# Graph attention layer on one core: the two column halves of an adjacency unit converted by one VectorE operation

## The reference

```python
xt = einsum('ni,hio->hno', x, W)                       # 8192 x 256 -> 4 heads x 64
src = einsum('hnf,hf->hn', xt, a[:, :64]);  dst = einsum('hnf,hf->hn', xt, a[:, 64:])
e = leaky_relu(src[:, :, None] + dst[:, None, :], 0.2)
attention = softmax(where(adj > 0, e, -inf), axis=2)
h_prime = einsum('hij,hjf->hif', attention, xt)
out = layernorm(x + h_prime.transpose(1, 0, 2).reshape(n, 256))
```

## Time and profile before

| | us |
|---|---|
| median of 3 runs | 2083.66 (2082.74 to 2085.49) |
| the profiled execution | 2083.11 |
| its span in the trace | 2081.3 |
| PE busy | 1982.0 (95%) |
| DVE busy | 1977.7 (95%) |
| ACT busy | 1955.4 (94%) |
| idle of ACT before signs (L539), total | 18.0 |
| idle of DVE before masks (L746), total | 41.1 |

### The profile page before, as it was taken

The page is one execution under the profiler, slowest core; times in us unless marked ns, Lnnn a source line. Parts: engine busy times, 40 slices in busy tenths (PEclk is TensorE's granted clock), DMA queues, the critical chain, the costliest instruction groups (busy, mean ns, idle before and its releaser), DMA issues.

```text
span 2081.3 us, 74808 instructions
## 1 busy us (share of the span) xinstructions
PE 1982.0 (95%) x33296; PEld 1949.5 (94%) x33296; DVE 1977.7 (95%) x2185; ACT 1955.4 (94%) x1983; POOL 142.1 (7%) x179
## 2 busy tenths in 40 slices
PE   7767999999999999999999999999999999999997
PEld 5567999999999999999999999999999999999997
DVE  3998999999999999999999999999999999999887
ACT  4477999999999999999999999999999999999995
POOL 0210000000020001000010000000010001001000
PEclk9889999999999999999999999999999999999998
DMA  8999999998988988989887979889988888834311
GB/s 295 331 369 380 293 279 264 264 249 236 253 239 248 271 246 232 254 236 285 237 257 227 282 234 254 240 244 274 252 238 245 266 256 230 229 89 125 88 49 42
DMA packets 289935, 498.59 MB, mean 240 GB/s; under 512 B 133008, under 2 KB 142224, under 8 KB 289616
## 3 DMA queue, kind: packets, MB, share of 16 engines
q1 hardware_dynamic: 285408, 477.96, 78.5%
q0 software_dynamic: 4080, 15.73, 2.3%
q10 hardware_dynamic: 128, 0.13, 0.0%
HBM read 438.83 MB, written 25.56 MB: 223 GB/s over the span
## 4 chain that ended last, share of the span: by engine, by line
ACT 48%; PE 35%; DVE 9%; issue 4%; DMA 3%; SPq 1%; POOL 0%; DVEq 0%; ACTq 0%; POOLq 0%
ACT big L539 46%; PE acc L1020 34%; DMA raw<-in_adj_dram 3%; DVE big L746 3%; DVE big L752 1%; DVE nat L660 1%; ACT big L581 1%; ACT big L587 1%; DVE nat L666 1%; DVE big L726 1%; PE acc L950 0%; DVE big L724 0%; DMA AT<-in_x_dram 0%; PE acc L960 0%; DVE AT L719 0%
## 5 line engine op out<-in xcount | busy, mean ns | idle before, releaser
L1020 PE MATMUL acc<-big 128*128 128x130 f16 x32768 | 1884.8, 220 | 45.0 <-DVE big L752 25.0
L1020 PEld LDWEIGHTS acc<-big 128*128 128x128 fp8e4 x32768 | 1871.3, 98 | 58.7 <-issue 57.1
L539 ACT ACTIVATE big<-big,d_all 128x1024 int8<-128x1024 f32 x1756 | 1848.7, 1152 | 18.0 <-PE acc L1020 17.9
L746 DVE SCALAR_TENSOR_TENSOR big<-big,AT 128x1024 uint32<-128x1024 uint32 x512 | 623.2, 1217 | 41.1 <-ACT big L539 38.9
L752 DVE SCALAR_TENSOR_TENSOR big<-AT,big 128x1024 uint32<-128x1024 uint32 x512 | 623.7, 1218 | 9.5 <-DVE big L746 0.5
L733 DVE TENSOR_SCALAR big<-big,d_all 128x1024 uint8<-128x1024 f32 x292 | 215.9, 746 | 0.0
L660 DVE TENSOR_SCALAR nat<-raw 128x2048 uint8<-128x2048 int32 x128 | 159.3, 1244 | 5.9 <-DMA raw<-in_adj_dram 5.6
L666 DVE TENSOR_SCALAR nat<-raw 128x2048 uint8<-128x2048 int32 x128 | 159.5, 1246 | 0.0
L483 POOL TENSOR_TENSOR wden<-big,ab 128x16 f32<-128x16 f32 x31 | 29.5, 950 | 886.2 <-DVE big L775 886.2
L673 DVE SCALAR_TENSOR_TENSOR nat<-nat 128x512 uint32<-128x512 uint32 x128 | 88.0, 688 | 0.0
L980 PE MATMUL acc<-big 128*128 128x256 f32 x256 | 62.1, 405 | 1.1 <-DVE AT L719 1.1
(11 more groups left out here) (64 smaller groups left out, 345.8 us busy)
## 6 DMA issues: line engine op xcount, KB each, us to landing
raw<-in_adj_dram SPq DMA_DIRECT2D x256, 1024.0 KB, 8.3
big<-v_parts SPq DMA_DIRECT2D x512, 260.0 KB, 6.6
v_parts<-big SPq DMA_DIRECT2D x16, 1040.0 KB, 7.1
big<-s_rows SPq DMA_DIRECT2D x32, 512.0 KB, 6.3
AT<-in_x_dram SPq DMA_DIRECT2D x16, 512.0 KB, 8.9
big<-in_x_dram POOLq DMA_DIRECT2D x8, 1024.0 KB, 11.2
out_dram<-big POOLq DMA_DIRECT2D x7, 1024.0 KB, 8.0
AT<-nat SPq DMA_TRANSPOSE x112, 8.7
```

The source lines that it names most:

```text
L539: return nc.scalar.activation(sgn[:, g % NB, :, b, :], sq[:, h % 2], ACT.Sign, bias=dflat[:, r:r + 1], scale=-1.0)
L746: nc.vector.scalar_tensor_tensor(out=word(sgn, g % NB), in0=word(sgn, g % NB), scalar=EDGE[g % 2], in1=edges(c, g), op0=ALU.bitwise_and, o ...
L1020: return nc.tensor.matmul(acc[:, k, o:o + 2 * VO], m[:, g % NB, t // 2, b, t % 2 * P:(t % 2 + 1) * P], Vr[:, v:v + 2 * VO], start=opens, s ...
```

## The change

From chunk 1 on (`all_columns`) one DVE operation with 4096 elements per partition converts both column halves of a unit, in step s = 4U+2. It writes 16 where an entry is above zero and 0 elsewhere, for both halves, into a new buffer `nat2` (in free words of `big`). Step 4U has no conversion any more. The merge stays in step 4U+3: it shifts the second half right by one bit (16 becomes 8) and ORs it into the first. The transposing DMA reads `nat2`. The waits on `raw` and on the earlier transpose, which `first_columns` had, now stand ahead of the one operation. The units of chunk 0 itself keep the two operations. The units for chunk 1, made during chunk 0, are converted in one operation at the place of the second one. New line numbers: mask 1 is L769, mask 2 L775, compares L756, the new conversion L685, the new merge L692, L775/L779/L805 are L798/L802/L828.

```diff
--- before.py
+++ after.py
@@ -83,6 +83,7 @@
         VR = 10240
         Vr = words(VR, 8320).bitcast(fp16)
         u = words(18560, 1040).rearrange("p (q v) -> p q v", v=VO)
+        nat2 = words(23696, 2048).bitcast(u8).rearrange("p (n v k) -> p n v k", n=2, v=2)
         y = [words(start, 2048).rearrange("p (t f) -> p t f", t=T) for start in (19600, 21648)]
 
 
@@ -189,14 +190,22 @@
         def edges(c, g):
             return AT[:, c % 2, g // 2]
 
-        def bits(c, n):
-            if c == 0:
-                return nat[:, n].rearrange("p (w z t) -> p z t w", z=2, t=2)
-            return nat[:, n].rearrange("p (z w t) -> p z t w", z=2, t=2)
+        def bits(n):
+            return nat[:, n].rearrange("p (w z t) -> p z t w", z=2, t=2)
 
         def columns(U, plane):
             k = U % 2 * 2
             return raw[:, k:k + 2, :, plane * CW:(plane + 1) * CW].rearrange("p z t w -> p z t w")
+
+        def bits_of_both(U):
+            return nat2[:, U % 2].rearrange("p v (z w t) -> p v z t w", z=2, t=2)
+
+        def columns_of_both(U):
+            k = U % 2 * 2
+            return raw[:, k:k + 2].rearrange("p z t (v w) -> p v z t w", v=2)
+
+        def joined(c, U):
+            return nat2[:, U % 2, 0] if c else nat[:, U % 2]
 
 
         def xt_of(n):
@@ -355,7 +364,7 @@
                 sp.wait_ge(merge_done, c * UN + U + 1)
                 sp.dma_start_transpose(AT[:, c % 2, U // 2, U % 2 * CW:(U % 2 + 1) * CW].bitcast(bf16)
                                        .rearrange("p (r i) -> p r i", i=P),
-                                       nat[:, U % 2].bitcast(bf16)).then_inc(turned[U % 2], 16)
+                                       joined(c, U).bitcast(bf16)).then_inc(turned[U % 2], 16)
 
             def load_x(g):
                 sp.dma_start(xg[g % NX], x_v[g]).then_inc(x_in[g % NX], 16)
@@ -648,30 +657,44 @@
 
 
 
-            def first_columns(c, U):
+            def raw_landed(c, U):
                 W = c * UN + U
                 dve.wait_ge(raw_in[U % 2 * 2], 16 * (W // 2) + 16)
                 dve.wait_ge(raw_in[U % 2 * 2 + 1], 16 * (W // 2) + 16)
+
+            def first_columns(U):
+                raw_landed(0, U)
+                if U > 1:
+                    dve.wait_ge(tp_done, U - 1)
+                dve.sem_inc(dve_passed, 1)
+                nc.vector.tensor_scalar(bits(U % 2), columns(U, 0), 0.0, BELOW[0], ALU.is_gt, ALU.add).then_inc(first_done, 1)
+
+            def last_columns(U):
+                if U:
+                    dve.wait_ge(merge_done, U)
+                nc.vector.tensor_scalar(bits(2), columns(U, 1), 0.0, BELOW[1], ALU.is_gt, ALU.add).then_inc(conv_done, 1)
+
+            def all_columns(c, U):
+                W = c * UN + U
+                raw_landed(c, U)
+                if W == UN:
+                    dve.wait_ge(*staged(NG - 1))
                 if W > UN + 1:
                     dve.wait_ge(turned[U % 2], 16 * ((W - UN) // 2))
-                elif W > 1:
-                    dve.wait_ge(tp_done, W - 1)
                 dve.sem_inc(dve_passed, 1)
-                nc.vector.tensor_scalar(bits(c, U % 2), columns(U, 0), 0.0, BELOW[0], ALU.is_gt, ALU.add).then_inc(first_done, 1)
-
-            def last_columns(c, U):
-                W = c * UN + U
-                if W:
-                    dve.wait_ge(merge_done, W)
-                nc.vector.tensor_scalar(bits(c, 2), columns(U, 1), 0.0, BELOW[1], ALU.is_gt, ALU.add).then_inc(conv_done, 1)
+                nc.vector.tensor_scalar(bits_of_both(U), columns_of_both(U), 0.0, 16.0, ALU.is_gt, ALU.mult).then_inc(conv_done, 1)
 
             def merge(c, U):
                 W = c * UN + U
-                dve.wait_ge(first_done, W + 1)
                 dve.wait_ge(conv_done, W + 1)
-                both = nat[:, U % 2].bitcast(u32)
-                nc.vector.scalar_tensor_tensor(out=both, in0=both, scalar=EDGE[0], in1=nat[:, 2].bitcast(u32),
-                                               op0=ALU.bitwise_and, op1=ALU.bitwise_or).then_inc(merge_done, 1)
+                both = joined(c, U).bitcast(u32)
+                if c:
+                    nc.vector.scalar_tensor_tensor(out=both, in0=nat2[:, U % 2, 1].bitcast(u32), scalar=1, in1=both,
+                                                   op0=ALU.logical_shift_right, op1=ALU.bitwise_or).then_inc(merge_done, 1)
+                else:
+                    dve.wait_ge(first_done, U + 1)
+                    nc.vector.scalar_tensor_tensor(out=both, in0=both, scalar=EDGE[0], in1=nat[:, 2].bitcast(u32),
+                                                   op0=ALU.bitwise_and, op1=ALU.bitwise_or).then_inc(merge_done, 1)
 
             def by_nodes(q):
                 dve.wait_ge(sdT_done, q + 1)
@@ -689,11 +712,11 @@
                 nc.vector.tensor_copy(sd[q % NS], acc[:, 4, :]).then_inc(sd_done, 1)
                 if q:
                     by_nodes(q - 1)
-            first_columns(0, 0)
+            first_columns(0)
             by_nodes(NQ - 1)
             dve.wait_ge(s_kept, 2 * NQ)
             nc.vector.tensor_reduce(mx[:, :], d_all[:, :, :].rearrange("p r h -> p h r"), AX.X, ALU.max).then_inc(mx_done, 1)
-            last_columns(0, 0)
+            last_columns(0)
             dve.wait_ge(M_done, 1)
             Mb = M[:, :].unsqueeze(1).broadcast_to([P, R, H])
             nc.vector.tensor_tensor(out=dM, in0=d_all[:, :, :], in1=Mb, op=ALU.subtract).then_inc(exp_in, 1)
@@ -764,9 +787,9 @@
                 for U in merged_with(g):
                     merge(0, U)
                 for U in first_columns_with(g):
-                    first_columns(0, U)
+                    first_columns(U)
                 for U in last_columns_with(g):
-                    last_columns(0, U)
+                    last_columns(U)
             lows(NG - 1)
 
             def high(p, part):
@@ -830,11 +853,13 @@
                                 if more or U < 0:
                                     merge(c + (U >= 0), U % UN)
                             for U in first_columns_at(c, s):
-                                if more or U < 0:
-                                    first_columns(c + (U >= 0), U % UN)
+                                if U < 0:
+                                    first_columns(U + UN)
                             for U in last_columns_at(c, s):
-                                if more or U < 0:
-                                    last_columns(c + (U >= 0), U % UN)
+                                if U < 0:
+                                    last_columns(U + UN)
+                                elif more:
+                                    all_columns(c + 1, U)
 
                         ec, eh = (c - 1, H - 1) if h == 0 else (c, h - 1)
                         ended = not (first and h == 0)
```

## The result

| | before | changed |
|---|---|---|
| median, us | 2084.43 (13 runs) | 2089.44 (2087.16 to 2092.04, 13 runs) |
| ratio, 95% interval | | 1.0026 (1.0018 to 1.0034) |
| the profiled execution, us (span) | 2083.11 (2081.3) | 2090.84 (2089.0) |
| DVE busy, us | 1977.7 | 1971.4 |

One of the 13 runs of the kernel before took 10596.7 us; the ratio leaves it out. The change costs 5.4 us of 2084 by the ratio, 3.8 to 7.1 by its interval. DVE has less to do than before and the kernel is slower.

The account below looks back on a forecast made before the run. The kernel was taken as bound by a loop through ACT, DVE and PE of 237.9 us per chunk; 0.37 for chunk 1 and 5 x 0.65 for chunks 2 to 6 gave +3.6, a median of 2087.2 us, range 2080.5 to 2091.0.

Parts of the forecast that it names:

- What bounds the kernel: Chunks 2 to 6: a loop of 139.2 on ACT, 0.1, 96.9 on DVE, 1.7 over PE, 237.9 us, becoming 238.6.
- The operation: DVE's conversion of a unit: 4096 elements in one operation cost 2.20 us instead of 2.27, saving 0.07 per unit.
- Merge and buffer: Merge in step 4U+3: same 512 words, shift instead of AND, 0 us, bounded by 0.05 either way.
- the loads: DMA loads for unit U+2: they wait for a conversion ending 1.07 us later but needed two steps later, cost 0.
- nothing is saved: Rival: the fused conversion still costs 2.27 us, 7.0 us more in all, so 2090.7; chance 0.16.
- The single rate: Rival: conversion falls to one element a cycle, 4.3 us per unit, about 2260 us in all; chance 0.03.
- the full fixed cost: Rival: fusing saves 0.16 us per unit, conversion 2.11, in all -0.8 us, 2082.9; chance 0.12.
- The place: Step 6 of head 1: 1.07 us more behind DVE's idle time, less 0.42 from six units, 0.65 later per period.
- The seams: PE's waits before steps 0 go, before 15 grow 0.6 to 0.9; rival: steps 15 not later, 2078, chance 0.13.
- The sum: Whole kernel: 0.37 us for chunk 1 plus 3.25 for chunks 2 to 6, together 3.6 us more.
- no change: Outcome for the whole kernel: time within 0.2%, that is 4.2 us, of before; chance 0.46.
- slower: Outcome for the whole kernel: more than 0.2%, that is 4.2 us, over before; chance 0.40.

Follow-up runs that it names:

- run 4: Changed kernel with every unit of chunks 1 to 6 converted in halves at the old places, new buffer and shifting merge kept: 2083.25 us, 0.9997 of the kernel before.
- run 1: Changed kernel with each unit's halves converted by two operations of 2048 elements, both in step 4U+2: 2093.0 us, 1.0044 of the kernel before.
- runs 2: Also `fused_in_step_4U`: changed kernel with the 4096-element operation in step 4U instead of 4U+2, chunks 1 to 6: 2087.11 us, 1.0017 of the kernel before.
- 5: Changed kernel with unit 5, or units 1 and 5, in halves at the old places: 2086.46 and 2085.61 us, 1.0016 and 1.0010 of the kernel before.
- 6 (its opposite): Changed kernel with units 4 and 5 in halves at the old places, all others fused: 2089.27 us, 1.0032 of the kernel before.
- 7 (four units): Changed kernel with units 0, 1, 4 and 5 in halves at the old places, the other twelve fused: 2084.72 us, 1.0010 of the kernel before.
- experiment 7: Changed kernel with units 0, 1, 4, 5, 9 in halves, without and with the residual's reload cut to one eighth: 2086.92 and 2081.93 us, 1.0016 and 0.9992.

## Why the prediction came out as it did

*What bounds the kernel* was right: a loop through ACT, DVE from its last idle time on, and PE's step 15 of head 2. Its length was forecast as 238.6 and measured as 238.57 in every period without a long stall. The second mask at its end comes 0.63 us later, forecast 0.65.

*The operation*: 2.20 us forecast, 2.20 measured. One reading was off by a hundredth: the two sizes of two-input operations are 0.52 apart (1.13 less 0.61) and not 0.53, which would have given 2.18. Merge and buffer were put at nothing, shown by run 4; so were the loads, and the fused operation indeed never waits for `raw` (0.0 idle before L685). The rival "nothing is saved" gave 2090.7, nearer to the measured median than the forecast's 2087.2, but its mechanism is refuted by the spacing and by run 1. The single rate (4.3) and the full fixed cost (2.11) are refuted by the same spacing.

*The place*: 1.07 us per period behind an idle time of DVE. The size was right, the explanation incomplete. I had one fixed place, before step 6 of head 1, and forecast an idle time of 0.7 there; it is 0.32, because the fused unit in step 2 had already made DVE late. My expectations for runs 2, 5, 6 (its opposite) and 7 (four units) failed for the same reason. The runs showed in its place: the loss arises at each step where DVE, short of half a conversion, reaches the signs, and the last such step before the seam counts.

*The seams*: as the forecast had it, waits before steps 0 gone and waits before steps 15 of heads 2 and 3 grown in return. DVE's busy time fell by 6.3 us where I wrote 8; the 112 spacings account for 7.8, and where the rest went I did not find.

*The sum*: +3.6 was low; the ratio says +5.4 with 3.8 as its lower end. The term that failed is one that the sum did not have: PE's stalls without a semaphore, put at nothing. The trace of before showed PE standing up to 1.4 us without a semaphore (1.27 in the row at 1189.60 above), and I took no note of it, since it was hidden. With the reload cut, the difference of the kernels' medians is 4.4, and their profiles have the copy of chunk 6 at 1771.24 and 1775.05, 3.8 apart, and spans 4.1 apart. That 3.8 is near the forecast partly by luck: chunk 1 gave 0.13 where I had 0.37 (copies at 581.71 and 581.84), and 0.35 of it is one period that still has a stall; the four others give 0.66 each, forecast 0.65. Behind the last copy come another 0.3, with PE's wait of 0.64 before the last step 15. With the full reload PE's stalls, which the changed kernel no longer hides, make 4 us of the profiled execution (2.75 and 1.6 in two periods). Of the median they would make the remaining 1 us, which the intervals do not separate from nothing. I had given "no change" (within 0.2%) 0.46 and "slower" 0.40; by the ratio of 1.0026 it is slower, though the interval's lower end, 1.0018, is within 0.2%.

*Open*: why the stalls are longer in the profiled execution of the changed kernel (2.2 to 2.5 us against 1.3 to 1.4), and why one with the old order was hit by 3.3 us (run 4) and others not; each is one profile. That the stalls end with a packet of instructions is read from all traces. That cutting the reload saves time is shown in one kernel (experiment 7). How the reload delays such a packet was not tried.

## What to carry to other kernels

Where three engines in a ring are equally full, a saving on one of them is worth only what survives until the next wait. Joining two operations in one place saves the fixed cost of one and moves the other's whole time behind whatever wait lies between them: here 0.07 us against 1.07. Before two operations are fused, look in the timeline for the idle times of that engine between the two places, with a margin of the moved operation's length, since the idle time moves with the change. And look for times in which an engine stands still without a semaphore: as long as the kernel has air there they cost nothing, and a change that takes the air brings them onto the clock.

## What the runs showed of the hardware

The conversion costs 1.135 us from start to start with 2048 elements and 2.20 with 4096, so 0.07 us do not depend on size, while the duration in the trace (1.24 and 2.29) is about 0.1 longer than the spacing. An output pattern with one dimension more (128x4x2x512) runs at the same rate.

PE stood still without a semaphore for 0.4 to 3.3 us in 49 places of the 14 traces, and each time it went on 2.3 to 2.8 us after the start of a 16 KB packet of the DMA queue `q8 instruction`. At the five matmuls where 40 of them stand, the stall begins 7 to 14 us after POOL has issued the reload, a transfer of 1 MB. With the transfer cut to 128 KB most of the time was gone in two pairs of profiles (4.4 to 1.0 us over five chunks in one kernel, 8.1 to 2.8 in the other), the kernel before scattered over 1.7 us where it had scattered over 4.0, and the kernel with five units in halves fell from 2086.92 to 2081.93 us. A full transfer does not always bring such a stall: `fused_in_step_4U` has none there.
